# A transformer layer with eight experts: expert weights loaded and used in alternating order, and one weight load moved behind another

## The reference

```python
x = x + attn_ref(layernorm(x), Wqkv, Wout)            # causal attention, 16 heads of 64
# second part, on z = layernorm(x):
ctx = relative_attention(z)                            # scores = ac + rel_shift(bd), causal
h = layer_norm(z + ctx @ Wo, g1, b1)
ff = relu(h @ Wff1 + bff1) @ Wff2 + bff2               # 1024 -> 4096 -> 1024
h = layer_norm(h + ff, g2, b2)
probs = softmax(h @ Wg); gate = probs.max(-1); disp = one_hot(probs.argmax(-1), 8)
hid = relu(einsum('bsd,edf->besf', h, We1) + be1)      # every expert on every token
eout = einsum('besf,efd->besd', hid, We2) + be2
moe = einsum('besd,bse->bsd', eout, disp) * gate
x = x + layer_norm(h + moe, g3, b3) @ Wout
```

## Time and profile before

| | us |
|---|---|
| runs shown | 8269.48 and 7792.02, midpoint 8030.75 |
| the profiled execution, its time | 7791.96 |
| its span, first to last instruction, slowest core (5) | 7790.9 |
| spans of the eight cores | 7761.9 to 7790.9 |
| PE busy (matmul) | 5736.3 (74%) |
| DVE, ACT, POOL busy | 1703.2, 1973.4, 499.6 |
| granted TensorE clock, mean | 0.853 |

### The profile page before, as it was taken

How to read it: one execution, slowest core, us unless ns; L and a number is a source line. 1 busy time by engine, 2 the same in 40 slices (tenths; PEclk the granted TensorE clock), 3 DMA queues, 4 the chain that set the end, 5 groups by cost and what they waited for, 6 DMA issues and landing times.

```text
span 7790.9 us, 118527 instructions; the slowest of 8 cores (7761.9 to 7790.9 us)
## 1 busy us (share of the span) xinstructions
PE 5736.3 (74%) x39984; PEld 3410.0 (44%) x39984; DVE 1703.2 (22%) x4197; ACT 1973.4 (25%) x4133; POOL 499.6 (6%) x942
## 2 busy tenths in 40 slices
PE   1946538534566247677998989989899898998954
PEld 1423313101444124444665656656556565665621
DVE  3266532355322232222000000000000000000025
ACT  0047300243355002222222222222222222222200
POOL 0000000132000000001010010100101001010000
PEclk9955669655688678888999999999999999999977
DMA  5000241344455551115042050420504205041022
GB/s 112 9 7 13 74 127 17 119 183 163 105 137 142 119 124 36 42 42 98 9 66 39 12 95 9 65 39 12 95 9 66 38 12 95 9 68 37 9 62 84
DMA packets 410954, 506.63 MB, mean 65 GB/s; under 512 B 113288, under 2 KB 279432, under 8 KB 410384
## 3 DMA queue, kind: packets, MB, share of 16 engines
q0 software_dynamic: 119472, 268.53, 17.5%
q1 hardware_dynamic: 212832, 171.78, 8.2%
q10 hardware_dynamic: 78080, 58.73, 2.3%
HBM read 524.10 MB, written 150.99 MB: 87 GB/s over the span
## 4 chain that ended last, share of the span: by engine, by line
PE 60%; DMA 16%; DVE 9%; issue 7%; ACT 5%; SPq 1%; ACTq 1%; DVEq 0%; POOL 0%; POOLq 0%
PE ps L1195 23%; PE ps L1181 22%; DMA W<-fWe 10%; PE ps L738 3%; PE ps L310 2%; PE ps L870 2%; PE ps L893 2%; DMA W<-fWff 2%; PE ps L761 1%; PE ps L599 1%; PE ps L1129 1%; DVE bst L614 1%; DMA bd<-bst 1%; PE ps L797 1%; PE ps L559 1%
## 5 line engine op out<-in xcount | busy, mean ns | idle before, releaser
L1195 PE MATMUL ps<-W,hidT 128*128 128x512 bf16 x9216 | 2030.8, 382 | 216.6 <-DMA W<-fWe 157.1
L1181 PE MATMUL ps<-mhw,W 128*128 128x256 bf16 x16384 | 1860.9, 272 | 36.7 <-DMA W<-fWe 32.7
L1187 ACT ACTIVATE hidT<-ps,c_be1c 128x256 bf16<-128x256 f32 x2048 | 969.4, 473 | 2908.7 <-PE ps L1181 2906.7
L1181 PEld LDWEIGHTS ps<-mhw,W 128*128 128x128 bf16 x16384 | 1470.2, 97 | 430.6 <-issue 47.0
L1195 PEld LDWEIGHTS ps<-W,hidT 128*128 128x128 bf16 x9216 | 900.9, 98 | 1331.1 <-issue 278.9
L1067 DVE SCALAR_TENSOR_TENSOR msel<-ps,c_maskg,msel 128x512 bf16<-128x512 f32 x256 | 192.2, 751 | 3682.4 <-PE ps L1195 3682.4
L133 POOL DMA_DIRECT2D W<-fWe x512 | 270.8, 533 | 3852.1 <-PE ps L1181 3342.2
L599 PE MATMUL ps<-rT,qv 64*128 64x512 bf16 x640 | 177.2, 602 | 272.7 <-DVE qv L585 190.5
L1181 PE MATMUL ps<-hw,W 128*128 128x256 bf16 x2048 | 252.5, 286 | 32.3 <-DMA hw<-h1T 32.0
L614 DVE CAST bst<-ps 128x512 bf16<-128x512 f32 x320 | 217.2, 691 | 212.0 <-PE ps L599 166.5
L609 ACT ACTIVATE bst<-ps 128x512 bf16<-128x512 f32 x320 | 190.5, 597 | 261.2 <-PE ps L599 177.9
(11 more groups left out here) (191 smaller groups left out, 3829.5 us busy)
## 6 DMA issues: line engine op xcount, KB each, us to landing
W<-fWe POOLq DMA_DIRECT2D x512, 256.0 KB, 12.5
bdsh<-bd SPq DMA_DIRECT2D x640, 96.0 KB, 2.6
bd<-bst POOLq DMA_DIRECT2D x64, 512.0 KB, 3.7
mhw<-h2T SPq DMA_DIRECT2D x64, 512.0 KB, 4.2
bd<-bst POOLq DMA_DIRECT2D x64, 384.0 KB, 3.2
bd<-bst POOLq DMA_DIRECT2D x64, 256.0 KB, 2.7
W<-fWff POOLq DMA_DIRECT2D x64, 256.0 KB, 14.1
bd<-zfill ACTq DMA_DIRECT2D x32, 256.0 KB, 4.5
```

Source lines behind the costliest of these rows:

```text
L1181: k.op("pe", lambda e, fc=fc, dc=dc, psj=psj: e.matmul(self.ps[psj][:, 0:256], W1[:, dc * FF + fc * 128: dc * FF + fc * 128 + 128], hT[:, ...
L1187: k.op("act", lambda e, fc=fc, psj=psj: e.activation(hid[:, fc * 256: fc * 256 + 256], self.ps[psj][:, 0:256], AF.Relu, bias=b1sb[:, boff ...
L1195: k.op("pe", lambda e, fc=fc, t2=t2, dh=dh, psj=psj: e.matmul(self.ps[psj][:, :], hid[:, fc * 256 + t2 * 128: fc * 256 + t2 * 128 + 128], ...
```

## The change

Two edits. In `build`, the 32 loads of Wff1 are issued after the eight loads of Wo instead of before them. In the expert loop, experts 1, 3, 5 and 7 load their weight groups in the order 3, 2, 1, 0 instead of 0, 1, 2, 3, and `ff_block` runs over `fc` from 31 down to 0 in both phases for them. The even experts and the dense block keep the rising order. Number and size of all loads and matmuls stay the same.

```diff
         W1, BW1g = self.alloc_w1(gW1)
-        self.load_w1(W1, BW1g, self.i["fWff1"].tensor, 0)
...
         k.dma("sp", g1s[:, :], self.i["g1"], writes=[Bg1s])
         k.dma("sp", b1s[:, :], self.i["b1"], writes=[Bb1s])
+        self.load_w1(W1, BW1g, self.i["fWff1"].tensor, 0)
...
-    def load_w1(self, W1, BW1g, src_tensor, base_off):
-        for fg in range(4):
+    def load_w1(self, W1, BW1g, src_tensor, base_off, rev=False):
+        fgs = list(range(4))
+        if rev:
+            fgs.reverse()
+        for fg in fgs:
...
-    def load_w2(self, W2, BW2g, src_tensor, base_off):
-        for fg in range(4):
+    def load_w2(self, W2, BW2g, src_tensor, base_off, rev=False):
+        fgs = list(range(4))
+        if rev:
+            fgs.reverse()
+        for fg in fgs:
...
         for ex in range(NE):
-            self.load_w1(W1, BW1g, self.i["fWe1"].tensor, ex * D * FF)
-            self.load_w2(W2, BW2g, self.i["fWe2"].tensor, ex * FF * D)
+            rv = (ex % 2 == 1)
+            self.load_w1(W1, BW1g, self.i["fWe1"].tensor, ex * D * FF, rev=rv)
+            self.load_w2(W2, BW2g, self.i["fWe2"].tensor, ex * FF * D, rev=rv)
...
-    def ff_block(self, W1, BW1g, W2, BW2g, hid, Bhid, hT, BhT, bias1):
+    def ff_block(self, W1, BW1g, W2, BW2g, hid, Bhid, hT, BhT, bias1, rev=False):
...
-        for fc in range(32):
+        fcs = list(range(32))
+        if rev:
+            fcs.reverse()
+        for fc in fcs:
...
-                for fc in range(32):
+                for idx, fc in enumerate(fcs):
...
-                        start=(fc == 0), stop=(fc == 31)),
+                        start=(idx == 0), stop=(idx == 31)),
                         reads=[Bhid, BW2g[fc // 8]], writes=[self.Bps[psj]],
-                        inc=(fc == 31))
+                        inc=(idx == 31))
```

More of the change, by code:

```diff
@@ L1061, in ff_moe_out @@
                 self.ff_block(W1, BW1g, W2, BW2g, hid, Bhid, w, Bw,
-                              (self.sb_p["be1c"], self.Bp["be1c"], ex * 32))
+                              (self.sb_p["be1c"], self.Bp["be1c"], ex * 32),
+                              rev=rv)
                 for t2 in range(2):
```

## The result

| | before | changed |
|---|---|---|
| profiled execution, span of the slowest core | 7790.9 us | 7871.9 us |
| its time | 7791.96 us | 7873.01 us |
| spans of the eight cores | 7761.9 to 7790.9 | 7848.9 to 7871.9 |
| median of all executions | 8079.7 us (10) | 8345.35 us (11) |
| ratio to before | | 1.0112, 95% interval 1.0079 to 1.0145 |

The change makes the kernel 1.1% slower. The forecast of 7884 us is 11 us above the profiled execution; the median of all executions, 8345, lies outside the stated range of 7820 to 7960.

The account below looks back on a forecast made before the run. The prediction took PE as the bound within an expert and the chain of 64 weight loads at changes of expert. 7791.96 + 152.1 - 60.2 gave 7884 us, range 7820 to 7960.

Parts of the forecast that it names:

- start of the chain: At each change of expert, POOL's first weight load waits for phase 1's 256th matmul instead of its 64th: 21.7 us later.
- chain, 64 loads: An expert's W1 and W2 loads, first issue to the matmuls needing the last group: stays 108 us, at a saturated rate.
- alternating order: Reversed group order delays the weight loads at all seven changes of expert: +152.1 us, bounds 122 and 170.
- Wo's eight loads, first issue to L310: Wo stage: 36.2 us to the eighth issue, as for the output weights, plus 4.4 us until its use.
- Wo before Wff1: Wo stage: L310 starts at 2565.9 instead of 2626.1, -60.2 us; bounds of the gain 46 and 66.
- falling loop in itself: Odd experts' blocks run from 31 down: same matmuls, banks and signals per block, so 0.
- the shadow in which PE's new waits lie: PE's waits in the next phase 1 (some 9 us) and phase 2 (some 35) are covered by the weight loads.
- the growth that the prediction named as a sign: Idle time of L1195 and L1181 waiting for expert weights grows by about 150 us together.
- The release of W2 as the bound: Rival at changes of expert: the later start costs nothing and only Wo counts, 7732 us; chance 0.07.
- Wo's gain eaten: Rival in the Wo stage: Wff1's traffic beside it delays five tiles by 12 us each, 7944 us; chance 0.08.
- POOL and DVE hindering each other: Rival in the Wo stage: DVE stands still during Wff1's 32 issues, adding 17 us, 7901 us; chance 0.06.
- stalls that cost more than their shadow: Rival at changes of expert: PE's pauses lower its clock, slowing the rest of phase 2 by 2 to 7 us; chance 0.07.

Follow-up runs that it names:

- the smaller dose: Kernel before, with expert ex loading and using its groups from group ex mod 4 on, going round; span 7836.5 us, dies 7817 against 7767 us.

## Why the prediction was right, and where not

**The time.** The sum of 7884 us was meant for an execution like the profiled one and came within 11 us of it. Some of that closeness is luck: the order was priced 11 us too high and Wo's gain 4 us too large, and the two errors partly cancel. Term by term, traces as means over the eight cores unless a core is named:

| term | forecast | measured |
|---|---|---|
| start of the chain, each change of expert | 21.7 us later | 29.6 - 7.9 = 21.7 us later |
| chain, 64 loads | unchanged, 108 | 106.3 against 107.7 |
| alternating order, seven changes | +152.1 | 7 x (506.0 - 485.8) = +141; alone, by dies, +143 to +147 |
| Wo's eight loads, first issue to L310 | 40.6 | 42.6 (41.5 to 44.7 by core) |
| Wo before Wff1 | -60.2 | 42.6 - 98.7 = -56; alone, by dies, -52 |
| falling loop in itself | 0 | 0 (ratio 0.9997) |

*The alternating order.* The mechanism held at each step: which group is released when, POOL's strict order, the shadow in which PE's new waits lie. The chain came out 1.4 us shorter, which makes 7 x 1.4 = 10 of the 11 us. PE's idle time came out at 28.8 + 8.3 = 37.1 us in the rows above (37.2 over all changes and cores) where 43.6 was forecast, so the growth that the prediction named as a sign, about 150 us, was 98 on the page. Besides the shorter chain, the rest of the delay is no idle time but slow matmuls between the stalls. In the rows above, 64 matmuls of L1192 take 8.68 and 10.01 us where those before the stalls take 7.32, and eight of L1206 take 3.40 and 3.57 where the first eight take 1.89. Windows of the changed kernel (columns as in the earlier trace rows) show the clock:

```profile
4488.00:4596.00 108.00, 69.91 (x409) 40.77 (x410) 3.00 (x4) 15.65 (x33) 33.83 (x64) 0.82 1.02 166
```

The mean grant over the whole chain is 0.82; over the same 108 us of the kernel before (4504 to 4612, core 5) it is 0.94. Without stalls the experts run at 1.00, which is the level of 2.4 GHz; after PE's pauses part of the matmuls run at the lower one, 1.2 GHz. This too lies in the chain's shadow: what counts is the time from the start of the 104 last matmuls to the next phase 1, and that is 24.5 us in both kernels (24.55 and 24.50, means of all 56 changes).

*Wo.* Direction and mechanism held, the gain was 4 us too large by the traces and 8 by dies. By the traces, half of the 4 us is the mis-sized term, the eight loads, 42.6 us and not 40.6: to the eighth issue they took 37.9 us on core 5 and 39.5 on core 7, not the 36.2 of the output weights, and the last was used 5.4 and 5.1 us after its issue, not 4.4. The other half is that the old stretch was read from core 5 alone, 100.8 us, where the mean of the eight cores is 98.7. It stays within the bounds given (gain of 46 to 66).

*The rivals.* The release of W2 as the bound falls: 145 us with the order alone, and the smaller dose costs its share. Wo's gain eaten falls: from the first L310 to the first load of Wff2 it takes 232.8 us in the changed kernel and 233.0 in the kernel before. That also disposes of POOL and DVE hindering each other in a way that costs time. In the changed kernel, from 2570 to 2640 us, while Wff1 is being issued, the DVE groups of the Wo stage are these:

```profile
L350 DVE TENSOR_TENSOR h1f<-h1f,s_b 128x1024 f32<-128x1024 f32 x4 | 4.9, 1226 | 0.5 <-DVE h1f L347 0.2
...
L690 DVE CAST h1b<-h1f 128x1024 bf16<-128x1024 f32 x4 | 2.8, 694 | 0.4
```

They are as long as without it (1226 and 694 ns). The exclusive lock of which the Trainium skill's page "SBUF — State Buffer", section "Who interferes with whom", speaks is not to be seen here, as the prediction had read from the earlier trace rows; four casts are few, and the length of the stage is the stronger evidence that it costs nothing here. The last rival, stalls that cost more than their shadow, falls too: 24.55 against 24.50 us is 0.4 us in all seven changes.

**The range.** This is where the prediction was wrong. Its range of 7820 to 7960 us was built around the profiled execution, with "about 0.4% on either side for runs of one kernel". The two times shown of the kernel before were 7792 and 8269 us, 6% apart. The prediction noted that its sum said nothing about that difference, and then gave a range without it. The step that failed is this 0.4%, the term for the spread between executions of one kernel. The runs showed a spread of 7 to 9% in its place: 7873 to 8444 us for the changed kernel, nine of eleven executions beside the profiled one at 8046 or above and their median at 8345, and 7790 to 8508 us for the kernel before. Either the range had to say for which executions it holds, or it had to reach up by the 6% already in view. Why the executions differ so much, no run here shows. The change itself (1.12% measured, 1.2% forecast) was within what was written.

## What to carry to other kernels

When a queue works strictly in order and a buffer is released piece by piece, load the pieces in the order in which they are released. Reversing the direction from block to block makes the first load wait for the last piece and everything behind it too, and here each microsecond of later start was about a microsecond of kernel time. Where a chain of loads ends last, look at how much work needs its last piece: turning a loop nest so that it is 32 matmuls instead of 104 gave about 100 us, twice what loading Wo first gave. And a load that is needed at once belongs ahead of one that is needed 200 us later.

## What the runs showed of the hardware

- The chain of 64 loads of 512 KiB took 103.6 to 114.1 us on every kernel with the usual `mhw` loads, under every order of groups and on every core read, on average 106.3 to 107.8, about 1.7 us a load. A hole of 4.25 us in its issue, with eight loads in flight, didn't lengthen it.
- A further load of 512 KB through SP's queue within such a chain lengthened it by 2.1 us (three lengthened it by 6.4), and leaving out two shortened it by 3.7 us, on all but 3 of 56 changes of expert.
- Stalls of 2 to 13 us between short bursts of matmuls brought the mean grant over 108 us down to 0.82; the bursts took about 7 us more there than at the full grant, which idle time alone doesn't show.
- Wff1's 32 loads beside the Wo stage (DMA share of 1.06 for 69 us) left its length as it was (232.8 against 233.0 us).
